# Sums of scattered rows in blocks: a shorter load of block numbers, unread products ahead of it, a wait for each group, and one group of one-hots in four on GpSimd

## The reference, cut to what matters

```
agg = segment_sum(x[src], dst)
h = (x + agg) @ W1 + b1          # W1: 128 -> 32
h = relu(h); h = bn(h)
h = h @ W2 + b2                  # W2: 32 -> 128
h = bn(h); leaky relu
```

## Time and profile before

| what | us |
|---|---|
| median of the three runs | 16785.31 |
| span of the profiled execution | 14549.9 |
| median less span | 2235.4 |
| the summing pass, in the span | 7021 to 7406 |
| the gather pass behind it | 7514 to 9690 |

### The profile page before, as it was taken

The page is one execution under the profiler, slowest core; times in us unless marked ns, Lnnn a source line. Parts: engine busy times, 40 slices in busy tenths (PEclk is TensorE's granted clock), DMA queues, the critical chain, the costliest instruction groups (busy, mean ns, idle before and its releaser), DMA issues.

```text
span 14549.9 us, 185642 instructions
## 1 busy us (share of the span) xinstructions
PE 5642.2 (39%) x42509; PEld 4641.8 (32%) x42510; DVE 6490.2 (45%) x25163; ACT 2071.4 (14%) x8809; POOL 10118.0 (70%) x10603
## 2 busy tenths in 40 slices
PE   7200002546655111111441111127888885444443
PEld 2000002333334100000441111127888884444442
DVE  9201113667765100000541111137888886656666
ACT  0000000000002111111010000015666662000000
POOL 4777777777774677777237777746777774777775
PEclk9655555768765555555555555559999996555555
DMA  4444449211112212211321111125555554333333
GB/s 109 127 126 140 127 141 81 53 50 52 52 51 61 54 46 46 46 46 44 92 52 20 20 20 20 20 51 132 131 131 131 131 130 113 80 80 79 80 80 86
DMA packets 1400883, 1138.59 MB, mean 78 GB/s; under 512 B 445673, under 2 KB 1261295, under 8 KB 1400143
## 3 DMA queue, kind: packets, MB, share of 16 engines
q1 hardware_dynamic: 1049493, 567.59, 16.8%
q0 software_dynamic: 335264, 554.74, 15.6%
q10 hardware_dynamic: 15778, 12.82, 0.3%
HBM read 871.76 MB, written 262.57 MB: 78 GB/s over the span
## 4 chain that ended last, share of the span: by engine, by line
POOL 58%; issue 19%; DVE 4%; PE 2%; DMA 1%; ACT 1%; DVEq 0%; SPq 0%; POOLq 0%; ACTq 0%
POOL work L807 34%; POOL rows_b L822 12%; POOL work L834 11%; DVE work L1887 2%; DMA x_tab<-work 0%; DVE work L1849 0%; DVE work L1855 0%; PE ps L1261 0%; DVE work L1801 0%; PE ps L1357 0%; PE ps L1224 0%; PE ps L1229 0%; DVE work L1941 0%; PE ps L1218 0%; DVE big L1632 0%
## 5 line engine op out<-in xcount | busy, mean ns | idle before, releaser
L807 POOL DMA_INDIRECT work<-q_tab,pay_a x1760 | 1673.5, 951 | 715.8 <-issue 535.1
L807 POOL DMA_INDIRECT work<-h_tab,pay_a x1760 | 1671.8, 950 | 673.5 <-issue 536.1
L807 POOL DMA_INDIRECT work<-in_x_dram,pay_a x1760 | 1709.4, 971 | 545.2 <-issue 536.0
L822 POOL DMA_INDIRECT rows_b<-work,big x1760 | 1706.7, 970 | 540.0 <-issue 536.2
L834 POOL DMA_INDIRECT work<-z_tab,work x1760 | 1662.8, 945 | 539.2 <-issue 536.0
L775 POOL DMA_INDIRECT edges_a<-work x1660 | 1607.4, 968 | 567.0 <-issue 508.7
L1625 DVE TENSOR_TENSOR big<-big,ps 128x128 f32 (+1 forms) x5280 | 1494.7, 283 | 940.8 <-PE ps L1127 531.9
L1868 DVE TENSOR_SCALAR work<-work,iota_p 128x512 bf16<-128x512 bf16 (+1 forms) x1320 | 560.3, 425 | 2220.0 <-PE ps L1240 1946.5
L1431 PE MATMUL ps<-work 128*128 128x129 f32 x3520 | 916.9, 441 | 1220.5 <-DVE work L1617 1220.5
L1127 PE MATMUL ps<-work 128*128 128x128 f32 x3520 | 749.3, 379 | 1376.2 <-DMA work<-in_x_dram,pay_a 995.5
L1431 PEld LDWEIGHTS ps<-work 128*128 128x128 f32 x3520 | 788.2, 329 | 1256.5 <-DVE big L1625 1162.3
(11 more groups left out here) (346 smaller groups left out, 12240.8 us busy)
## 6 DMA issues: line engine op xcount, KB each, us to landing
work<-lo_rows SPq DMA_DIRECT2D x1320, 128.0 KB
work<-edges_a SPq DMA_DIRECT2D x440, 256.0 KB
work<-in_edge_attr_dram SPq DMA_DIRECT2D x166, 640.0 KB, 5.1
rows_b<-work SPq DMA_DIRECT2D x80, 550.0 KB, 7.5
work<-rows_b SPq DMA_DIRECT2D x110, 400.0 KB, 3.2
work<-in_x_dram,pay_a POOLq DMA_INDIRECT x1760
rows_b<-work,big POOLq DMA_INDIRECT x1760
work<-z_tab,work POOLq DMA_INDIRECT x1760
```

The costliest lines, as they stand in the source:

```text
L807: pool.indirect_dma_start(out=ring[:, at:at + width], out_offset=None, in_=table, in_offset=bass.IndirectOffsetOnAxis(ap=pay[:, e, 1:2], a ...
L822: pool.indirect_dma_start(out=rows_b, out_offset=bass.IndirectOffsetOnAxis(ap=pos_b[:, s * G + j:s * G + j + 1], axis=0), in_=message[:, k ...
```

## The change

Five things change, all in the summing pass. The rest of the diff is bookkeeping: two semaphores with one use each (`s_lot`, `s_blkmm`) become one, `s_side`, which makes room for the new `s_ohp`, and the count of groups that the gather pass waits for becomes `SUMMED` = 440 + 110 * 3 = 770.

1. A step of `chunk_sums` is one chunk and not two. It loads 16 block numbers and not 32.
2. Ahead of each load stand five matmuls (KEEP) of 512 columns into PSUM bank 7, whose result nobody reads.
3. TensorE waits for each group of one-hots, and not for four at once. So it has four waits and four increments of `begun` for a chunk.
4. Of the four groups of a chunk VectorE makes the first three (MINE).
5. GpSimd makes the fourth.

```diff
+        MINE = (0, 1, 2)
+        SUMMED = GROUPS + TILES // CHUNK * len(MINE)
+        KEEP = 5
...
+            for c in range(TILES // CHUNK):
+                pool.wait_ge(z1.payload, c + 1)
+                wait(pool, s1.mm, 4 * c + (GROUPS - 4))
+                for j in range(G):
+                    at = len(MINE) * G + j
+                    ins = pool.tensor_scalar(onehot_h[:, c % 2 * 4 + len(MINE), j], iota_h[:, :], lo_chunk[:, c % 5, at:at + 1], None, ALU.is_equal)
+                ins.then_inc(s_ohp, 1)
...
             def chunk_sums(s, k, u):
 
-                bl = load_blocks(ONLY_PE, blk_b, s, 2 * CHUNK)
-                for h in range(2):
-                    c = 2 * s + h
-                    pe.wait_ge(s1.oh, c * 4 + (GROUPS + 4))
+                for _ in range(KEEP):
+                    pe.matmul(ps[:, 7, :].rearrange("p (a q) -> p a q", q=P), lhsT=before_h[:, :],
+                              rhs=iota_h[:, :].unsqueeze(1).to_broadcast([P, 4, P]), start=True, stop=True, skip_group_check=True)
+                bl = load_blocks(ONLY_PE, blk_b, s, CHUNK)
+                for n in range(CHUNK // G):
+                    if n in MINE:
+                        pe.wait_ge(s1.oh, s * len(MINE) + (GROUPS + n + 1))
+                    else:
+                        pe.wait_ge(s_ohp, s + 1)
                     pe.sem_inc(begun, 1)
-                    for n in range(CHUNK // G):
-                        for j in range(G):
-                            for f in range(3):
-                                m = pe.matmul(ps_flat[:, bass.ds(bl[h * CHUNK + n * G + j] * H, H)], lhsT=onehot_h[:, 4 * h + n, j],
-                                              rhs=chunk[:, (2 * k + h) % 5, n * G + j, f * H:(f + 1) * H], start=False, stop=True, skip_group_check=True)
-                        m.then_inc(s1.mm, 1)
+                    for j in range(G):
+                        for f in range(3):
+                            m = pe.matmul(ps_flat[:, bass.ds(bl[n * G + j] * H, H)], lhsT=onehot_h[:, k % 2 * 4 + n, j],
+                                          rhs=chunk[:, k % 5, n * G + j, f * H:(f + 1) * H], start=False, stop=True, skip_group_check=True)
+                    m.then_inc(s1.mm, 1)
...
-            run_steps(pe, TILES // CHUNK // 2, 5, 0, chunk_sums)
+            run_steps(pe, TILES // CHUNK, 10, 0, chunk_sums)
...
+                if k % 4 not in MINE:
+                    return
                 wait(dve, s1.mm, s + (GROUPS - 7))
```

More of the change, by code:

```diff
@@ L469, in gnn_program @@
         s_pay = [sem(f"s_pay{k}") for k in range(3)]
-        s_lot, s_lotc, s_lost, s_blkf, s_blkmm, s_pb = (sem(n) for n in
-            ("s_lot", "s_lotc", "s_lost", "s_blkf", "s_blkmm", "s_pb"))
+        s_side, s_lotc, s_lost, s_blkf, s_ohp, s_pb = (sem(n) for n in
+            ("s_side", "s_lotc", "s_lost", "s_blkf", "s_ohp", "s_pb"))
         got = [sem(f"got{h}") for h in range(RING)]
@@ L1170, in _ @@
                 m = pe.transpose(ps[0:w, 4 + c // 4, (c % 4) * P:(c % 4 + 1) * P], pay_a[:, c * w:(c + 1) * w, 0], ident[:, :])
-            m.then_inc(s_lot, 1)
+            m.then_inc(s_side, 1)
             for s in range(49, HIST):
@@ L1195, in _ @@
                 m = pe.matmul(ps[:, 4 + c, 0:TILES // 4], lhsT=ones[0:1, :], rhs=blk_f[:, c * (TILES // 4):(c + 1) * (TILES // 4)], start=True, stop=True)
-            m.then_inc(s_blkmm, 1)
+            m.then_inc(s_side, 1)
             laps(pe, (END + 12) // RING, GROUPS // RING, sum_step)
@@ L1270, in gather_sum @@
                     g = s * (CHUNK // G) + n
-                    pe.wait_ge(p2.oh, g + (2 * GROUPS + 1))
+                    pe.wait_ge(p2.oh, g + (SUMMED + 1))
                     pe.sem_inc(begun, 1)
@@ L1687, in _ @@
             group(49)
-            dve.wait_ge(s_lot, 1)
+            dve.wait_ge(s_side, 1)
             for c in range(16):
@@ L1772, in _ @@
                 group(s)
-            dve.wait_ge(s_blkmm, 1)
+            dve.wait_ge(s_side, 2)
             group(END + 12)
```

## The result

The changed kernel takes 16864.36 us (median of four runs, 16853.93 to 16881.42), the kernel before beside it 16782.17 us (four runs, 16775.68 to 16787.63). The ratio is 1.0051, with a 95% interval of 1.004 to 1.0063: slower by 82 us. The forecast was 16875 us, slower by 90.

The account below looks back on a forecast made before the run. It took TensorE's sequencer to bound the summing pass: 3.03 us for four groups, 1.31 for the load and 0.03 for products make 4.37 us a chunk against 3.485. With small savings that gave +90 us, 16875 us, range 16845 to 16965.

Parts of the forecast that it names:

- work of the sequencer is what counts: Summing pass: TensorE's sequencer, by register operations, waits and loads, sets the pace, and the array has time to spare.
- Four waits: TensorE in the summing pass: a wait and an increment for each group, +0.71 us a chunk, +78 us over 110 chunks.
- Loads of 16: TensorE's block-number loads in the summing pass: halving saves nothing, surroundings come twice; +0.14 us a chunk, +16 us in all.
- Products: Five unread matmuls ahead of each load in the summing pass: run beside the load, cost only their issue, 0.03 us a chunk.
- The sum: A chunk of the summing pass takes 4.37 us against 3.485, +97 us; less ends and clock, +90 us.
- GpSimd's passes and all else are the same: Outside the summing pass: GpSimd's DMA passes and everything else keep their time, so nothing is added for them.
- GpSimd's one-hot: Fourth group's one-hots on GpSimd in the summing pass: 0.37 us each with its gap, 1.5 us for four; upper bound 0.70.
- Rival C: Summing pass: VectorE and GpSimd exclude each other, a chunk wants 5.2 us, pass 570 us, time 16970; chance 6%.
- A: Summing pass: the array paces the matmuls, so the higher clock makes it faster, -145 us, 16640; chance 8%.
- B: Summing pass: steps shrink with the clock by a quarter or so, time within 33 us of before; chance 5%.
- D: Summing pass: the products block the load, a chunk takes 2.1 us more, 6.5, time 17100; chance 3%.
- I add the difference to the median: Whole kernel: runs take 2235 us more than the profiled span, cause unknown, so +90 us goes onto the median 16785.3.

Follow-up runs that it names:

- f2: The kernel before with five unread products ahead of each load of 32 numbers; summing pass 385.3 us, time 16610.07 us (one run) against 16628.92.
- e2: The changed kernel without the unread products (KEEP = 0); summing pass 476.3 us, ratio 1.0081 to the kernel before.
- g1: The changed kernel with one matmul for a tile and not three; summing pass 476.3 us, time 14677.35 us (one run).
- e4: The changed kernel with all 16 one-hots of a chunk on VectorE, none on GpSimd; summing pass 478.7 us, ratio 1.0052 to the kernel before.
- f1: The kernel before with a wait and an increment for each group, nothing else of the change; summing pass 462.2 us, ratio 1.0049 to the kernel before.
- e1: The changed kernel with two waits and increments for a chunk and not four; summing pass 425.6 us, ratio 1.0051 to the kernel before.
- e3: The changed kernel with one load of 32 numbers for two chunks, led by five products; summing pass 463.9 us, time 16687.94 us (one run).
- b1: The kernel before with one wait and increment for eight groups and block numbers stored times 32; summing pass 355.3 us, ratio 0.9981 to the kernel before.
- b2: The kernel before with one wait for eight groups, no increment of begun, block numbers stored times 32; summing pass 345.1 us, ratio 0.9974 to the kernel before.
- e5: The changed kernel with 15 unread products ahead of each load and not 5; summing pass 562.6 us, time 16792.1 us (one run).
- a0_again: The changed kernel once more, unchanged, on a chip with stalls; summing pass 478.0 us, ratio 1.005 to the kernel before.
- r1: The kernel before with only the change's bookkeeping of semaphores; summing pass 384.3 us, ratio 0.9999 to the kernel before.

## Why the prediction was right

**Who sets the pace.** The step "work of the sequencer is what counts" holds. f2 and e2 change the clock, e2 and g1 the array's work, e4 VectorE's work, all by much, and none moves the pass by over 1.7 us. f1, e1, e3, b1 and b2 change what the sequencer does, and the pass follows by the price of it.

The sequencer's own instructions say the same without any subtraction of runs. From one register operation to the next, with nothing but matmuls between, the median is 124 ns in before, after, f1, e1, e2, g1 and e5 alike: with three matmuls or one, at 0.50 of the clock or at 1.00. It is 115 in b1 and b2, whose operation is 9 ns shorter. With a wait and its increment between the two it is 368, so 244 more, and 275 in the first chunks, which are written out and don't work out the value: 151 for the semaphore instruction, 93 for the register operation. With a load of 16 and its wait between them it is 1659. In after a chunk is one of these, three of 368 and twelve of 124, 4.25 us by the medians, and 4.36 by the means, where 4.34 was measured.

**Four waits.** +78 us as summed; f1 shows 78.1 for it alone.

**Loads of 16.** +16 us in the sum; e3 shows 14, half of the products with it. Its working (a price for each number, surroundings twice) holds.

**Products.** +3 us in the sum; f2 and e2 show 1.2 to 1.7. The clock left 0.50 as expected and was worth nothing in the pass. Behind it line 1351's transposes took 2.95 us and not the 5.50 of the earlier trace rows, 2.6 of the 3 us allowed for.

**The sum.** 0.885 us a chunk were predicted and 0.849 came: 78.1 + 14 + 1.2 = 93.3, where the pass grew by 93.4. (That they agree to 0.1 is chance: e3's 14 holds some of the products too.) The runs grew by 82 us, and by 86 in a0_again. The forecast of +90 is within 8 us of both.

**What it had at nothing: GpSimd's DMA passes.** "GpSimd's passes and all else are the same" does not hold on the chip without stalls. There e2, the change without its products, is slower by 114 us (1.0081), when the stretch from the last `rows_b` DMA to the first of the gather pass has only 90 of them. The first two passes of DMAs (lines 778 and 810, in before 775 and 807) have 28 more: 2143.0 and 2256.2 us against 2126.1 and 2245.4. On chips with stalls the single DMAs are longer too (967 ns in a0_again, 958 in r1), but the two passes are not, 2439.8 and 2553.0 us against 2441.3 and 2550.7. So the mechanism in the summing pass was right, but that the whole came out so near +90 is in part luck: it depends on the chip that the times were taken on.

**The mis-sized term: GpSimd's one-hot.** "I take 0.37 with its gap: 1.5 us for four" was wrong. The view by line, in the summing pass of after:

```profile
L833 POOL TENSOR_SCALAR work<-iota_h,lo_chunk 128x128 bf16<-128x128 bf16 x440 | 259.9, 607 | 218.3 <-PE ps L1276 207.8 <-ACT work L931 5.4 <-issue 5.1
L1904 DVE TENSOR_SCALAR work<-iota_h,lo_chunk 128x128 bf16<-128x128 bf16 x1320 | 238.9, 254 | 220.8 <-PE ps L1276 218.1
```

Four take 2.34 us. The value came from the select, nearest by size; the upper bound, 0.70 for an operation with two inputs, was the nearer one. A smaller miss is VectorE's twelve at 0.168: they take 2.26 to 2.28 us, 0.189 each, so VectorE is busy for 249 us and not 225 (the prediction's own 2.1 us a chunk would have made it 231). Neither cost time, as TensorE waits for neither.

**Rival C was nearer than its 6% said.** It was to decide from 0.57 us for GpSimd's one-hot, and 0.585 (2.34 / 4) is past that. With 0.18 for line 1898, a chunk of both, one after the other, would be 2.27 + 0.18 + 2.34 = 4.79 us, more than the 4.34 that it took. It did not occur because the engines don't exclude each other: in 43 us of the pass both make one-hots. 91 of VectorE's lie wholly inside one of GpSimd's, and take 264 ns on the mean where those apart from it take 249. GpSimd's take 690 ns on the mean when VectorE is busy for nearly all of one (19 of them), and 602 when it isn't at all. So each slows the other a little. The Trainium skill ("SBUF — State Buffer", section "Who interferes with whom") has the one that comes second "fully block" where VectorE's operation is in a mode with both of its ports. This case's trace shows nobody blocked; whether VectorE's one-hots ran in such a mode no run here shows. The long mutual delay of the earlier trace rows was with other operations, f32 and with two inputs.

**Rivals A, B and D** fall by the same runs. A needed matmuls that shrink with the clock: the groups start 0.74 to 0.79 us apart at either level. B needed the same in part. D needed a load that waits for the products: after's load starts 0.05 us behind the first of five, e5's in the first third of 15.

**The median less the span.** The step "I add the difference to the median" held, though the cause of the difference was open then. It is nearly all time in GpSimd's DMA passes that depends on the chip, ahead of the summing pass and behind it, and not in it.

## What to carry to other kernels

Count what an engine's sequencer does between the instructions that show as busy: each register operation, wait, increment and register load has its price there, and in this kernel neither a faster clock nor a free array paid any of it back. The chain and the releasers may name another engine all the same; two rows with the same register operations and a different number of matmuls tell which of them paces. Where a loop is bound so, gather the waits, drop increments that nothing needs, keep numbers in memory in the form in which an address wants them, and give helpers for other engines no credit until the sequencer has been made faster.

## What the runs showed of the hardware that was not expected

**The same kernel differs by 2200 us between chips**, all in passes of indirect DMAs on GpSimd. Before takes 14553.69 us on one chip and 16622.77 to 16782.17 on three others. On those the profile has GpSimd wait before the DMAs of line 807 for "remote", another core or an unknown queue: 665 times, 1132 us in all, in r1_names_only, and never in before's profile. What it is stays open. The summing pass is the same on both kinds (r1 384.3 us, before 384.1), but the difference between two kernels need not be: e2, with a pass of 476.3 us, costs 114 us on the quiet chip, and a0_again, with one of 478.0, costs 86 on another.

**An indirect DMA's time on GpSimd follows the program, by 1%.** Line 775 (778 with the change) is the same code in each of these, and runs long before the summing pass. Before, f1_group_waits, e1_two_waits and after, in this order (min, median and longest in ns):

```profile
L775 POOL DMA_INDIRECT edges_a<-work x1660: 952/958/1870, 184.3 to 2309.4; - x185
```

```profile
L775 POOL DMA_INDIRECT edges_a<-work x1660: 952/958/1866, 184.4 to 2308.8; - x185
```

```profile
L778 POOL DMA_INDIRECT edges_a<-work x1660: 963/967/1863, 183.5 to 2325.2; - x185
```

```profile
L778 POOL DMA_INDIRECT edges_a<-work x1660: 965/971/1912, 183.0 to 2630.5; - x185
```

The 9 ns of e1 come in this pass and, by its median, in the next (952 against 944), 3420 DMAs in all: some 30 us. That is about what e1, e2 and g1 take on the quiet chip beyond their longer summing pass (e1: 75 us in all, 41 of them in the stretch from the last `rows_b` DMA to the first of the gather pass). It is not the renamed semaphores (r1: 958), and without GpSimd's one-hots about half of it is left (e4: 962). On chips with stalls it does not lengthen the passes, as said above. f2, whose GpSimd code is that of before, has 962 as well. What in the program sets it stays open.

**GpSimd makes a 128x128 one-hot in bf16 in 0.60 us**, VectorE one each 0.17 to 0.19, so even a quarter of them keeps GpSimd busy as long as VectorE with the other three (260 and 239 us).
